# Router logits and null scores with swapped matmul operands, in a four-layer recurrent transformer kernel

## What is computed

```python
kv = jnp.concatenate([jnp.broadcast_to(null_kv, (b, 1, DIM_HEAD)), kv], axis=1)
sim = jnp.einsum('bhid,bjd->bhij', q, kv)     # then mask, softmax
```

## Time and profile before

| | |
|---|---|
| time, median of 3 runs | 2109.11 us (2106.24 to 2113.43) |
| the profiled execution | 2105.85 us, span 2104.1 us |
| mean granted TensorE clock | 0.953 |
| TensorE busy | 90% of the span |
| VectorE, POOL, ScalarE busy | 66%, 59%, 46% |

### The profile page before, as it was taken

The page is one execution under the profiler, slowest core; times in us unless marked ns, Lnnn a source line. Parts: engine busy times, 40 slices in busy tenths (PEclk is TensorE's granted clock), DMA queues, the critical chain, the costliest instruction groups (busy, mean ns, idle before and its releaser), DMA issues.

```text
span 2104.1 us, 31556 instructions
## 1 busy us (share of the span) xinstructions
PE 1903.2 (90%) x9838; PEld 1263.6 (60%) x9838; DVE 1382.9 (66%) x3816; ACT 962.5 (46%) x1993; POOL 1231.4 (59%) x1600
## 2 busy tenths in 40 slices
PE   5999999999885899999999898988789999888985
PEld 3555556665584566666666466867556665545554
DVE  7787777787434766666666455445577888766733
ACT  2435444444454545554555434445334445444443
POOL 1668977777644357777777700011256777788754
PEclk9999999999997899999999988999889999999997
DMA  5335122132152424443444120000312223222233
GB/s 142 85 92 144 54 70 60 34 80 51 52 160 66 107 66 102 100 100 81 108 96 96 38 83 21 1 12 1 90 36 72 54 55 85 63 70 69 54 110 100
DMA packets 125967, 155.56 MB, mean 74 GB/s; under 512 B 21880, under 2 KB 66200, under 8 KB 125544
## 3 DMA queue, kind: packets, MB, share of 16 engines
q1 hardware_dynamic: 121704, 145.42, 27.7%
q0 software_dynamic: 4096, 8.12, 1.2%
HBM read 47.84 MB, written 17.40 MB: 31 GB/s over the span
## 4 chain that ended last, share of the span: by engine, by line
PE 61%; POOL 12%; DVE 10%; issue 10%; ACT 4%; DMA 1%; SPq 1%; POOLq 0%; DVEq 0%; ACTq 0%
PE P L822 60%; POOL acc L1564 4%; POOL yd L1581 3%; DVE P L1955 2%; POOL pr L1542 2%; POOL xg L1572 2%; POOL acc L1561 1%; ACT pr L1328 1%; DVE mx L1944 1%; DVE mx L1965 1%; PE P L902 1%; DMA xg<-xs,sidx 1%; DVE bst L1856 0%; DVE qB L1917 0%; PE P L849 0%
## 5 line engine op out<-in xcount | busy, mean ns | idle before, releaser
L1564 POOL TENSOR_TENSOR acc<-acc,pr 128x512 f32<-128x512 f32 (+3 forms) x768 | 677.1, 904 | 62.6 <-ACT pr L1328 38.2
L1328 ACT ACTIVATE pr<-P 128x512 f32<-128x512 f32 (+1 forms) x768 | 396.5, 567 | 315.7 <-PE P L822 313.5
L822 PE MATMUL P<-pr,vt 128*64 128x512 f32 (+3 forms) x2304 | 435.7, 504 | 17.0 <-POOL pr L1542 16.5
L822 PE MATMUL P<-qA,kA 128*128 128x512 f32 (+2 forms) x1024 | 395.9, 390 | 28.3 <-ACT pr L1328 23.0
L1542 POOL TENSOR_SCALAR_AFFINE_SELECT pr<-pr 128x256 f32<-128x256 f32 x384 | 156.9, 408 | 383.6 <-ACT pr L1328 271.2
L822 PE MATMUL P<-qB,kB 128*128 128x512 f32 (+2 forms) x1024 | 369.0, 366 | 0.0
L822 PE MATMUL P<-kA,qA 128*128 128x512 f32 (+2 forms) x1152 | 313.6, 374 | 19.9 <-DVE rd L2001 5.9
L822 PEld LDWEIGHTS P<-qA,kA 128*128 128x128 f32 x1024 | 194.7, 190 | 154.2 <-issue 74.2
L1944 DVE TENSOR_REDUCE mx<-P 128x1 f32<-128x512 f32 x384 | 244.6, 683 | 56.4 <-PE P L822 55.7
L822 PEld LDWEIGHTS P<-pr,vt 128*64 128x64 f32 x2304 | 143.6, 139 | 224.5 <-issue 153.6
L822 PEld LDWEIGHTS P<-kA,qA 128*128 128x128 f32 x1152 | 194.0, 195 | 126.0 <-issue 70.7
(11 more groups left out here) (331 smaller groups left out, 2759.9 us busy)
## 6 DMA issues: line engine op xcount, KB each, us to landing
qA<-hq SPq DMA_DIRECT2D x384, 128.0 KB
kA<-stage SPq DMA_DIRECT2D x168, 128.0 KB, 2.3
qB<-qB SPq DMA_DIRECT2D x96, 128.0 KB, 2.4
kB<-stage SPq DMA_DIRECT2D x84, 128.0 KB, 2.4
nr<-null_share SPq DMA_DIRECT2D x64, 128.0 KB, 2.9
yd<-in_c_zero SPq DMA_DIRECT2D x32, 128.0 KB, 2.6
w<-in_L_W SPq DMA_DIRECT2D x16, 256.0 KB, 4.8
xg<-xg SPq DMA_DIRECT2D x24, 129.0 KB
```

The lines of the kernel that those rows point to most:

```text
L822: return P.matmul(out, lhs, rhs, start=start, stop=stop)
L1328: S.activation(a.pr[slot][:, r, 512 - wide:512], m.bank[b][:, 512 - wide:512], AF.Exp, scale=0.125).then_inc(s.free[b], 1)
L1564: G.tensor_tensor(acc[:, sl], acc[:, sl], pt[:, sl], ALU.add).then_inc(s.acc, 1)
```

## The change

The operands of both products are swapped. The weights become stationary and 512 rows of x move. As a matmul then has 8 (16) output partitions, several groups are put side by side in one bank: the weights stand in the middle of a tile of zeros (`m.wr`, 56 columns; `a.U`, `a.Ul`, 112 columns), and the window of 32 (96) columns that is loaded is shifted by 8 (16) for each group, so that group g lands on partitions 8g to 8g+7 and adds zeros elsewhere. All four groups of a router (both of a null-score item) are one accumulation in one bank. ScalarE copies the 32 rows that are of use to SBUF in two pieces (`lt`). Then a new item, `rt_q` (`snt`), transposes them back, four transposes of 32 x 128 into another bank, and one copy puts them in the old layout.

In the list, `[rt_w], [rt_p 0], [rt_p 1], [rt_p 2], [rt_p 3]` becomes `[rt_w], [], [rt_p], [], [rt_q]`; `snt` for half 0 stands behind the second group of maxima, for half 1 two groups of `late` behind sn 1. The zeros are written in `null` and, once, in layer 0's `rt_w`.

```diff
 def router_order(L):
-    out = [[("rt_w", L)]] + [[("rt_p", L, g)] for g in range(4)]
+    out = [[("rt_w", L)], [], [("rt_p", L)], [], [("rt_q", L)]]
...
+        if L == 3 and g == 1:
+            od.add("snt", L, 0)
...
-    attention_order(od, 3, router_order(3), [[("ald", 3)], [("rtld", 3)]] + late_norm(3) + [[("sn", 3, 1)]])
+    attention_order(od, 3, router_order(3), [[("ald", 3)], [("rtld", 3)]] + late_norm(3) + [[("sn", 3, 1)], [], [("snt", 3, 1)]])
...
# TensorE
-                for n in range(8 * k[1], 8 * k[1] + 8):
-                    sl = slice(n * 128, n * 128 + 128)
-                    t = mm3(ps[:, n * 16:n * 16 + 16], m.xh[:, sl], m.xl[:, sl], a.U[:], a.Ul[:], True, True)
+                for i in range(2):
+                    at, tk = slice(16 - 16 * i, 112 - 16 * i), slice(1024 * k[1] + 512 * i, 1024 * k[1] + 512 * i + 512)
+                    t = mm3(ps[0:96, :], a.U[:, at], a.Ul[:, at], m.xh[:, tk], m.xl[:, tk], i == 0, i == 1)
+                t.then_inc(s.full[b], 1)
+            elif kind in ("snt", "rt_q"):
+                w.wait_ge(*pl.emptied(*(("sn",) + k if kind == "snt" else ("rt_p",) + k)))
+                w.wait_ge(s.free[b], uses)
+                for j in range(4):
+                    t = P.transpose(ps[:, 32 * j:32 * j + 32], m.R[L].lt[j // 2][:, 128 * (j % 2):128 * (j % 2) + 128], m.ident[0:32, 0:32])
...
             elif kind == "rt_p":
-                L, g = k
                 w.wait_ge(s.rt_v, od.step["rt_w", L])
-                w.wait_ge(*pl.emptied("xT", L, g))
-                w.wait_ge(s.free[b], uses)
-                for n in range(4):
-                    sl = slice(g * 512 + n * 128, g * 512 + n * 128 + 128)
-                    t = mm3(ps[:, n * 8:n * 8 + 8], m.xh[:, sl], m.xl[:, sl], m.wrh[:], m.wrl[:], True, True)
+                w.wait_ge(*pl.emptied("xT", L, 3))
+                w.wait_ge(s.free[b], uses)
+                (wh, wl), at = m.wr, lambda g: slice(24 - 8 * g, 56 - 8 * g)
+                for g in range(4):
+                    tk = slice(512 * g, 512 * g + 512)
+                    t = mm3(ps[0:32, :], wh[:, at(g)], wl[:, at(g)], m.xh[:, tk], m.xl[:, tk], g == 0, g == 3)
...
# ScalarE
             elif kind == "sn":
                 w.wait_ge(s.full[b], f)
-                S.copy(m.A[3].sn[:, 8 * k[1]:8 * k[1] + 8].rearrange("p n h -> p (n h)"), ps[:, 128 * k[1]:128 * k[1] + 128]).then_inc(s.free[b], 1)
+                S.copy(m.R[3].lt[0], ps[0:32, 0:256])
+                S.copy(m.R[3].lt[1], ps[0:32, 256:512]).then_inc(s.free[b], 1)
+            elif kind == "snt":
+                w.wait_ge(s.full[b], f)
+                S.copy(m.A[3].sn[:, 8 * k[1]:8 * k[1] + 8].rearrange("p (i j) h -> p j i h", i=2),
+                       ps[:, 0:128].rearrange("p (j i h) -> p j i h", j=4, i=2)).then_inc(s.free[b], 1)
+            elif kind == "rt_p":
+                w.wait_ge(s.full[b], f)
+                S.copy(m.R[k[0]].lt[0], ps[0:32, 0:256])
+                S.copy(m.R[k[0]].lt[1], ps[0:32, 256:512]).then_inc(s.free[b], 1)
...
# VectorE
-                V.tensor_tensor(m.wrl[:].bitcast(FR), m.R[L].wr[:], m.wrh[:], ALU.subtract).then_inc(s.rt_v, 1)
-            elif kind == "rt_p":
-                L, g = k
-                w.wait_ge(s.full[b], f)
-                V.tensor_copy(m.R[L].lg[:, 4 * g:4 * g + 4, :].rearrange("p n e -> p (n e)"), ps[:, 0:32]).then_inc(s.free[b], 1)
+                wh, wl = m.wr
+                if L == 0:
+                    for half in m.wr:
+                        for sl in (slice(0, 24), slice(32, 56)):
+                            V.tensor_scalar(half[:, sl].bitcast(FR), m.ident[:, sl], 0.0, None, ALU.mult)
+                V.tensor_tensor(wl[:, 24:32].bitcast(FR), m.R[L].wr[:], wh[:, 24:32], ALU.subtract).then_inc(s.rt_v, 1)
+            elif kind == "rt_q":
+                L, = k
+                w.wait_ge(s.full[b], f)
+                V.tensor_copy(m.R[L].lg[:].rearrange("p (g j) e -> p j g e", g=4),
+                              ps[:, 0:128].rearrange("p (j g e) -> p j g e", j=4, g=4)).then_inc(s.free[b], 1)
```

More of the change, by code:

```diff
@@ L73, in settle @@
         self.stream.wait_ge(self.sem, self.n)
-BANKS = {"xT": ("misc", 1), "rt_p": ("aux", 1), "rt_t": ("aux", 1), "rt_off": ("aux", 1), "rt_t2": ("aux", 1),
+BANKS = {"xT": ("misc", 1), "rt_p": ("aux", 1), "rt_q": ("aux", 1), "rt_t": ("aux", 1), "rt_off": ("aux", 1), "rt_t2": ("aux", 1),
          "rt_rows": ("aux", 1), "bis": ("aux", 1), "bis_room": ("aux", 1), "bis_off": ("aux", 1),
-         "q": ("aux", 1), "k": ("aux", 1), "max": ("aux", 1), "rows": ("aux", 1), "sn": ("aux", 1), "v": ("aux", 1),
+         "q": ("aux", 1), "k": ("aux", 1), "max": ("aux", 1), "rows": ("aux", 1), "sn": ("aux", 1), "snt": ("aux", 1), "v": ("aux", 1),
          "score": ("score", 2), "pv0": ("pv", 1), "close": ("aux", 1), "out": ("aux", 1), "nbias": ("aux", 1),
@@ L526, in memory @@
     m.wk = sb(ctx, "wk", [128, NT, 2])
-    m.wrh, m.wrl = sb(ctx, "wrh", [128, 8]), sb(ctx, "wrl", [128, 8])
+    m.wr = [sb(ctx, f"wr{i}", [128, 56]) for i in "hl"]
     m.R, m.A, m.E = {}, {}, {}
@@ L547, in router @@
             r.wT, r.wte = m.xf[0:8].rearrange("p n d -> p (n d)"), sb(stack, "wte", [128, NT, 8])
+            r.lt = [m.xf[0:32, 2 * i:2 * i + 2, :].rearrange("p n d -> p (n d)") for i in range(2)]
             return r
         r.m1, r.m2 = sb(stack, "m1", [128, 256]), sb(stack, "m2", [128, 256])
+        r.lt = [r.m1[0:32, :], r.m2[0:32, :]]
         r.Ls, r.Lg = sb(stack, "Ls", [128, 128]), sb(stack, "Lg", [128, 128])
@@ L658, in memory @@
         with ExitStack() as layer:
-            first = weights(layer, *((1024,) * 4 if L != 3 else (1024, 1024, 64, 64, 512, 512, 64, 512, 64, 16, 16, 16, 16)))
+            first = weights(layer, *((1024,) * 4 if L != 3 else (1024, 1024, 64, 64, 512, 512, 64, 512, 64, 112, 112, 16, 16)))
             m.R[L] = router(layer, L)
@@ L1344, in run @@
                 w.wait_ge(s.rt_in, {0: 16 * 5, 1: 16 * 7, 3: 16 * 13}[L])
-                S.copy(m.wrh[:].bitcast(FR), m.R[L].wr[:]).then_inc(s.rt_wh, 1)
+                S.copy(m.wr[0][:, 24:32].bitcast(FR), m.R[L].wr[:]).then_inc(s.rt_wh, 1)
             elif kind == "rt_sm":
@@ L1963, in run @@
                 w.wait_ge(*pl.emptied(*od.last_max[k]))
-                w.wait_ge(*pl.emptied("sn", 3, bb))
+                w.wait_ge(*pl.emptied("snt", 3, bb))
                 chain(V.tensor_tensor(big.bitcast(FR), big, null, ALU.max))
@@ L1981, in run @@
                 chain(V.tensor_tensor(a.Us[:], a.Us[:], a.Ut[:], ALU.add))
-                chain(V.tensor_copy(a.U[:].bitcast(FR), a.Us[:]))
-                V.tensor_tensor(a.Ul[:].bitcast(FR), a.Us[:], a.U[:], ALU.subtract).then_inc(s.null_v, 1)
+                chain(V.tensor_scalar(a.U[:].bitcast(FR), m.ident[:, 0:112], 0.0, None, ALU.mult))
+                chain(V.tensor_scalar(a.Ul[:].bitcast(FR), m.ident[:, 0:112], 0.0, None, ALU.mult))
+                chain(V.tensor_copy(a.U[:, 16:32].bitcast(FR), a.Us[:]))
+                V.tensor_tensor(a.Ul[:, 16:32].bitcast(FR), a.Us[:], a.U[:, 16:32], ALU.subtract).then_inc(s.null_v, 1)
             elif kind == "dsum":
@@ L2033, in run @@
                 r = m.R[L]
-                w.wait_ge(*pl.emptied("rt_p", L, 3))
+                w.wait_ge(*pl.emptied("rt_q", L))
                 if L == 3:
```

## The result

The changed kernel takes 2091.3 us (median of six runs, 2088.22 to 2096.66); the kernel before, run beside it, takes 2106.43 (six runs, 2104.62 to 2113.43). The ratio is 0.9924, 95% interval 0.9905 to 0.9943: faster by 0.76%; the two medians by themselves differ by 15.1 us, which is 0.72%. The forecast was 2094.0 with a range of 2086 to 2105 and 15.1 us of gain; it lies 2.7 us above the measured median because it starts from the first three runs of before (median 2109.11), and all six have 2106.43.

The account below looks back on a forecast made before the run. TensorE was taken as the bound, paced by narrow matmuls' weight loads and a halved clock. Terms 3.7 + 4.0 + 4.0 + 1.6 + 2.1 - 0.3 = 15.1 us took 2109.11 to 2094.0, range 2086 to 2105.

Parts of the forecast that it names:

- The share of the clock: Routers and null scores: of the 15.1 us gain, 6.3 rest on the clock staying up, leaving 8.8 without it.
- the first rival: Clock falls all the same despite wide logits: 6.3 us of gain lost, about 2100 us; chance 0.17.
- The added wait (1.07 us): Layers 1 and 3, between rt_p and rt_q: TensorE stands 1.07 us for matmul tail, ScalarE's two copies and handings over.
- Layer 3's first group (0.6 of 1.43): Layer 3's router, ahead of close: removing the first group gains only 0.6 of 1.43 us, as close waits for POOL.
- Layer 0's 1.7: Layer 0's router, q and close: 4.15 us would become 2.4 if wide logits keep the clock up, 1.7 back.
- layer 1's 2.4: Layer 1's router, close and sixteen weighted sums: 5.79 us at half clock would become 3.3 to 3.4, gain 2.4.
- Layer 3's clock (0.8, by VectorE's slack of 0.77): Behind layer 3's router: the clock would give 1.5 to 2 us, but VectorE waits only 0.77, so 0.8 counted.
- sn 0 (1.6 us): First null score, at half clock: six wide matmuls 2.64 and four transposes 0.85 replace 24 narrow matmuls, gain 1.6 us.
- sn 1 (2.1): Second null score: 0.7 us gained from wide matmuls and 1.4 from the clock behind it.
- The preparation of the padded weights (0.3): Layer 2 and before layer 0's low half: six added VectorE operations cost 0.3 us, bounded at 0 to 2.3.
- VectorE takes the gain back: Behind the routers, VectorE's queue decides: about half of their 11.7 us gain goes, 2099 to 2107 us; chance 0.20.
- A lower rate with 32 weight columns: The 48 wide matmuls with 32 weight columns take four times 0.233 us: 33.5 us more, 2127.5; chance 0.03.

Follow-up runs that it names:

- early: The changed kernel with rt_p one step sooner, two empty steps between it and rt_q: 0.9927 of the kernel before, 2087.63 us.
- before_b: The unchanged kernel before, profiled a second time with no edit: span 2108.0 us, against 2104.1 in the forecast's profile.
- again: The changed kernel once more, no edit, for a second profile: 0.9928 of the kernel before, 2089.34 against 2103.81 us.
- null_only: The changed kernel with the routers put back to narrow matmuls, null scores as changed: 0.9986 of the kernel before, 2099.84 us.
- after: The changed kernel in its first profile, against the kernel before: median 2091.3 us, ratio 0.9924, profiled span 2090.2 us.
- extra_wide: The changed kernel with 18 extra wide logit matmuls ahead of each router's twelve, results overwritten: 0.9976 of the kernel before, 2099.39 us.
- extra_narrow: The changed kernel with 36 extra narrow 8-column matmuls ahead of each router's twelve, results overwritten: 1.0015 of the kernel before, 2108.6 us.
- spread: The kernel before with its four groups of narrow logit matmuls set apart by other work: 1.0026 of the kernel before, 2110.52 against 2104.38 us.

## Why the prediction was right, point by point

- **TensorE's issue was the bound: shown.** Extra wide matmuls cost their issue time one for one at three places, so nothing else decides there. Twelve wide ones take 2.77 us in layer 0 (2.8 in the sum), the transposes 0.36 (0.45). In layer 3 the three groups of 6.92 became 4.01 (1528.43 to 1532.44), 2.9 gained for 2.6.
- **The share of the clock was put too low.** The prediction gives 8.8 us to the pace and 6.3 to the clock. But the 6.92 us of layer 3's last three groups were themselves at the lower clock (0.192 each). At the 0.105 of full clock these 36 matmuls are 3.8 us, no more than the 4.01 of what replaced them, so the gain there is the clock's. By this estimate some 5.7 us of the sum are pace and 9.4 clock, and the price of the first rival, 8.8 us left, was too high as well.
- **The added wait (1.07 us): right in place, a little large.** From the pitch's end of the last wide matmul (742.43 + 0.23) to the first transpose it is 0.88. The two copies overlap and take 0.63 together in layer 3 (1531.40 to 1532.03), not 0.7; the rest is that tail and handings over were counted at 0.36 and come out smaller. In layer 0 there is none, as said; `early` removed it and got its size back.
- **Layer 3's first group (0.6 of 1.43): right.** Close waits for POOL, and the lead at its start grows by 0.68 us (9.42 to 10.10).
- **The clock: that narrow matmuls bring the fall is shown, its size varies.** Fifteen routers with wide logits, in five profiles, have no fall behind the logits; twelve with narrow ones have eleven. Adding 36 narrow matmuls brought it back at all three places. But a fall has one of several lengths and now and then stays out. Layer 0's 1.7 was nothing in one profile with narrow logits, and layer 1's 2.4 would be 0.8 against before_b (4.57 - 1.61 leaves 3.0 of 4.0 for the whole place). The forecast took these terms from one execution as if they were fixed.
- **Layer 3's clock (0.8, by VectorE's slack of 0.77): right, though the table of places shows 1.7.** Up to 1550.9, where the place ends, TensorE's lead grows by 1.7 us (13.01 at 1545.45, 14.71 at 1550.9). VectorE's grows by 0.9: its copy of the logits stands 13.01 us earlier (1545.56 to 1532.55, behind a wait of 3.30 for the transposes), its maxima 13.91 us (1551.81 to 1537.90), now without a wait. TensorE then gives the difference back: it waits 0.26 us for VectorE's `mx`, where before had no wait, and 1.66 instead of 1.36 for the exponential of ScalarE, which itself waits for VectorE. The lead at 1560.48 is 13.93. The same 0.8 us go between 1550.9 and 1560.48 in all five profiles with wide logits. So 0.8 to 0.9 of the 1.7 stays. Rows of TensorE and ScalarE in the changed kernel, then the one of ScalarE in before, 13.93 us later:

```profile
1541.01 0.50 PE L826 MATMUL P<-kA,qA 128*128 128x512 f32 x1 [0.26 <-DVE mx L1974]
...
1545.80 0.21 ACT L1329 ACTIVATE mx<-mx 128x8 f32<-128x8 f32 x1 [4.54 <-DVE mx L1985]
```

```profile
1559.73 0.21 ACT L1310 ACTIVATE mx<-mx 128x8 f32<-128x8 f32 x1 [3.73 <-DVE mx L1966]
```

- **sn 0 (1.6 us): mis-sized, some 2.7.** The six wide matmuls at the lower clock took 2.65 (2.64 in the sum), and 2.46 is gained at once. The term that was too large is the 0.85 for its transposes at half clock. They stand at 1479.50 to 1479.86 in the changed kernel, take 0.36, and the clock is 1.00 there, as the fall has a pause from 1478.4 to 1481.8 where before's goes on to 1495.1. What the lead loses by them it has back within 2 us in this pause. The 3.2 of the table for again, null_only and early hold 0.4 from ahead of sn 0, time lost to a fall in other work that TensorE has back in its wait for VectorE. **sn 1 (2.1):** 2.45 to 2.5.
- **The preparation of the padded weights (0.3):** no cost is seen ahead of layer 0's router, where after has a lead of 0.01; in layer 2 it can't be told from the differences between executions.
- **The total.** The places gave 18.8 us in the profile, 18.0 without the 0.8 that goes back behind 1550.9, for 15.4 in the sum; the stretches between them took 4.3 back in that profile and 3.0 in the next, which lies within what two executions of the unchanged kernel differ by there. So the close hit of the total, 15.1 for 15.1, is in part luck: two deviations that cancel.

**The rivals.** *The clock falls all the same* is out for the routers: in after the records of the clock have no fall from 717.2 to 1201.9, and in extra_wide the stretch 746 to 752, with wait, transposes and close in it, is at 1.00. The Trainium skill, "TensorE: Matmul & The Clock Gate", "PE-mode transpose", says that transposes don't count as busy in the same way for the clock; a quiet stretch of 0.72 us and four small transposes in 0.36 was not enough to make this matter here. The same page's section "Why this matters for your kernels" puts drops in mid-kernel down to idle gaps. In extra_narrow the clock was halved from 745.7 on, with TensorE busy for 10.00 of the 10 us from 742 to 752, so gaps aren't the only cause in this kernel. *VectorE takes the gain back* is out as a loss of half the gain, by extra_wide's one-for-one cost; what it does take is the 0.8 us behind layer 3's router. *A lower rate with 32 weight columns* is out by the pitch of 0.231, and for 96 columns likewise.

What stays open: why narrow logits lower the clock in 11 places and not in the twelfth; which property of the narrow matmuls does it; whether the change makes the fall between 1494 and 1511 more likely; and whether `early` is better in whole runs.

## What to carry to other kernels

Where a product has few columns on one side, let the wide operand move: here 48 matmuls with 8 moving columns cost 0.104 to 0.11 us each at full clock, with a weight load of 128 columns for each, twelve with 512 do the same work at 0.23, and the transposes back are small if their copies are hidden behind two steps of other work. An engine that is busy for the whole of a stretch may still lose its clock: look at the granted clock of the stretch behind narrow matmuls as well as of the matmuls. And before a term is taken from one profile, look at whether a second execution has it; a gain is read safest as the lead of the same instruction just ahead of a place and just behind it, and once more behind the next wait for another engine: in layer 3, half of the 1.7 us that the clock seemed to give was gone 10 us later.

## What the runs showed of the hardware beyond what I expected

- Two executions of the same program can differ by 1.6 us at one router by the length of one fall of the clock (1.61 in layer 1, 1.62 in layer 3), and by 8.2 us over all the stretches between the places.
- Falls went from four places, behind the three routers and sn 1, and the time at the lower clock hardly sank: 198 us in the profile of before, 194 in that of after, since falls in other stretches came, went or changed in length. The mean granted clock (0.953, 0.954) says nothing of the change; the stretches do.
- Setting narrow groups apart by about 0.8 to 1 us of wide matmuls does not keep the clock up: in spread it fell in layers 0 and 3, and in layer 1 behind the last group.
- 36 narrow matmuls, 3.8 us of issue, cost this kernel 5.5 to 7.2 us at a router; 18 wide ones, 4.2 us of issue, cost 4.1 to 4.2.
